# Batch 0's by-key scores on row strips, and the deviation factors on the projected queries

## What is computed

```python
q = split_heads(layernorm(x) @ Wq + bq); k = split_heads(y @ Wk + bk); v = split_heads(y @ Wv + bv)
w = softmax(einsum('bhqd,bhkd->bhqk', q, k) / sqrt(32)); o = merge_heads(w @ v) @ Wo + bo
x = x + tanh(g_xattn) * o
z = layernorm(x); s = max(amax(|z|), 1e-6) / 127; zq = clip(round(z / s), -128, 127)
x = x + tanh(g_ffn) * ((zq @ Wq8.T) * s * w_scale + bias)
```

## Time and profile before

| | |
|---|---|
| median of 3 runs | 812.34 us (811.54 to 814.0) |
| profiled execution | 812.89 us |
| its span, first to last instruction | 811.1 us |
| PE busy | 780.3 us (96%) |
| mean granted TensorE clock | 0.987 |
| POOL, DVE, ACT busy | 66%, 67%, 75% |

### The profile page before, as it was taken

One profiled execution on the slowest core, in us unless ns is written; L12 is line 12 of the kernel. 1 busy time (PEld: TensorE's weight loads), 2 busy tenths in 40 slices (PEclk: granted clock), 3 DMA queues, 4 the chain that ended last, 5 costly groups with the idle time before them and its releaser, 6 DMA issues.

```text
span 811.1 us, 16246 instructions
## 1 busy us (share of the span) xinstructions
PE 780.3 (96%) x5890; PEld 533.0 (66%) x5890; DVE 539.8 (67%) x849; ACT 610.8 (75%) x844; POOL 533.9 (66%) x554
## 2 busy tenths in 40 slices
PE   8897799999999999999999999999999999999996
PEld 6665366667667766766766676676667677666563
DVE  5864567567666756767676676766667665656568
ACT  5773577878687887768778686877868787787785
POOL 4844447585685857578485756949576694845588
PEclk9998899999999999999999999999999999999999
DMA  8998698779768786986878797686779768656722
GB/s 289 309 269 243 198 277 241 221 196 308 230 186 254 223 261 197 267 243 212 259 214 239 197 304 228 190 268 210 260 200 281 221 175 252 188 161 186 208 67 103
DMA packets 119503, 183.21 MB, mean 226 GB/s; under 512 B 37632, under 2 KB 47232, under 8 KB 117376
## 3 DMA queue, kind: packets, MB, share of 16 engines
q1 hardware_dynamic: 92352, 133.33, 53.3%
q10 hardware_dynamic: 27072, 48.84, 22.6%
HBM read 123.91 MB, written 58.22 MB: 225 GB/s over the span
## 4 chain that ended last, share of the span: by engine, by line
PE 76%; POOL 5%; issue 5%; DVE 4%; DMA 3%; ACT 3%; SPq 2%; ACTq 1%; DVEq 0%; POOLq 0%
PE bank_b L428 24%; PE bank_a L428 16%; PE scores L483 7%; PE sum_ps L510 6%; PE scores L502 6%; PE pv_ps L514 6%; PE bank_a L558 4%; PE bank_b L558 2%; SPq L231 2%; PE bank_a L533 1%; DMA k_rows<-k_parts 1%; PE scores L428 1%; DMA rstd_rows<-ln_rstd 1%; POOL o_lo_end L1585 1%; POOL x_rstd L1559 1%
## 5 line engine op out<-in xcount | busy, mean ns | idle before, releaser
L1585 POOL TENSOR_TENSOR o_lo<-on,o_hi 128x512 fp32r<-128x512 f32 x48 | 62.3, 1298 | 139.0 <-ACT o_hi L915 139.0
L1236 DVE TENSOR_REDUCE row_max<-scores 128x16 f32<-128x1920 f32 x64 | 137.9, 2155 | 22.6 <-PE scores L483 22.4
L895 ACT ACTIVATE probs<-scores 120x2048 f32<-120x2048 f32 x64 | 120.2, 1877 | 28.9 <-PE scores L502 28.9
L1248 DVE SCALAR_TENSOR_TENSOR q_parts<-bank_b,bq_c,q_parts 128x512 fp32r<-128x512 f32 x45 | 33.5, 744 | 108.9 <-ACT q_parts L857 108.9
L1540 POOL TENSOR_TENSOR xt<-xt,rstd_b 128x512 f32<-128x512 f32 x60 | 92.3, 1576 | 12.3 <-DMA xt<-in_x_t 10.6
L1593 POOL TENSOR_TENSOR x<-x,gbias_r 128x512 f32<-128x512 f32 x64 | 83.0, 1300 | 20.2 <-ACT cen L921 19.1
L483 PEld LDWEIGHTS scores<-k_sb,q_sb 32*128 32x128 f32 x1952 | 60.5, 187 | 52.4 <-issue 46.5
L1581 POOL TENSOR_TENSOR x<-x,gbo_r 128x512 f32<-128x512 f32 x64 | 83.3, 1313 | 0.8 <-DMA x<-in_x 0.7
L502 PE MATMUL scores<-q_stack,k_stack 128*120 128x512 f32 x256 | 72.8, 406 | 8.3 <-DMA k_stack<-k_rows 7.6
L1598 POOL TENSOR_TENSOR x<-x,u_sb 128x512 f32<-128x512 f32 x56 | 72.7, 1299 | 4.7 <-DVE u_sb L1324 4.5
L428 PE MATMUL bank_b<-xt_hi,wq_hi 128*128 128x512 f32 x188 | 74.9, 399 | 0.0
(11 more groups left out here) (235 smaller groups left out, 1953.1 us busy)
## 6 DMA issues: line engine op xcount, KB each, us to landing
q_stack<-q_rows ACTq DMA_DIRECT2D x183, 256.0 KB, 4.4
q_rows<-q_parts SPq DMA_DIRECT2D x62, 512.0 KB, 5.4
xt<-in_x_t SPq DMA_DIRECT2D x16, 1024.0 KB, 7.9
x<-in_x SPq DMA_DIRECT2D x64, 256.0 KB, 4.5
out_x<-x SPq DMA_DIRECT2D x61, 256.0 KB, 3.2
x_in<-in_x SPq DMA_DIRECT2D x60, 256.0 KB, 5.1
k_stack<-k_rows SPq DMA_DIRECT2D x96, 120.0 KB, 4.6
k_rows<-k_parts SPq DMA_DIRECT2D x28, 240.0 KB, 2.9
```

Of the source, the lines that this page charges most:

```text
L895: act.activation(probs[0:KEYS], scores[0:KEYS], ACT.Exp, scale=SCALE).then_inc(p_ready, 1)
L1236: dve.tensor_reduce(row_max[:].rearrange("p (t r) j -> p r t j", r=ROWG)[:, :, :, j], scores[:, :, 0:QT * KEYS].rearrange("p r (t k) -> p ...
L1585: pool.tensor_tensor(o_lo[i % 2][j], on[:], o_hi[i % 2][j].bitcast(F32), ALU.subtract).then_inc(o_split, 1)
```

## The change

Three things are changed.

1. **Batch 0's by-key scores without HBM.** `scores_by_key0(j)` takes the queries and keys of batch 0 as they lie, four heads on four strips of 32 rows. Three passes of four products (high by high, high by low, low by high) and a fourth with the maxima (8 rows of each strip, picked by `pick0`) add up in the four PSUM banks. The stores and stacks of batch 0 go away (`store_q(0, j)`, `stack_q(0, j)`, `stack_k(0, h)`), and `copy_max` and `spread_max` of batch 0 with them; the high parts are taken by ACT (`split_high0`), the low parts by DVE (`split_low0`). `low_k(0, 0)` to `low_k(0, 3)` are still needed for batch 1 and move later; SP's list ahead of step 1 is written anew.
2. **x unscaled in every batch.** `scale_x` is gone from POOL. DVE multiplies the projected queries with the deviations in the PSUM bank (`scale_q(n, j, bank)`), between `project_q` and `bias_q`; `bias_q` now waits for `q_scaled`.
3. **Places.** In the first quarter of a step, `scale_q(b, 0)` and `split_low(b, 0)` stand ahead of `quant_max(e, 2)`. In the third, `scale_q(b, 2)` stands between `quant_max(m, 0)` and `quant_max(m, 1)`. On PE the wait for `q_split(b, 0)` moves behind `quantised_layer(e, 1)`.

```diff
             def bias_q(n, j, bank):
...
-                act.wait_ge(q_done, nth(n, DT, j))
+                act.wait_ge(q_scaled, nth(n - 1, DT, j))
...
+            def scores_by_key0(j):
+                pe.wait_ge(qk0_split, nth(j, 2, 1))
+                q, k = q0_parts(j), k0_parts(j)
+                for p, (a, b) in enumerate(((0, 0), (0, 1), (1, 0))):
+                    for r in range(ROWG):
+                        pe.matmul(scores[0:KEYS, r], k[a][STRIPS[r]], q[b][STRIPS[r]], start=p == 0, stop=False)
...
+                for r in range(ROWG):
+                    rows = slice(r * DH, r * DH + PAIR)
+                    ins = pe.matmul(scores[0:KEYS, r], pick0[rows, j:j + 1].broadcast_to([PAIR, KEYS]), max0_t[rows],
+                                    start=False, stop=True)
...
+            def scale_q(n, j, bank):
+                dve.wait_ge(q_done, nth(n, DT, j))
+                if n == 1:
+                    dve.wait_ge(rstd1_copied, 1)
+                    dve.tensor_tensor(bank[:], bank[:], rstd1, ALU.mult).then_inc(q_scaled, 1)
+                else:
+                    dve.wait_ge(rstd_landed, 16 * (n - 1))
+                    by_tile = bank[:].rearrange("q (t p) -> q t p", t=QT)
+                    dve.tensor_tensor(by_tile, by_tile, rstd_b[:].rearrange("q (p t) -> q t p", t=QT),
+                                      ALU.mult).then_inc(q_scaled, 1)
...
                 if is_batch(m):
                     quant_max(m, 0)
+                if is_batch(b):
+                    scale_q(b, 2, bank_a)
+                if is_batch(m):
                     quant_max(m, 1)
                     quant_factors(m, 0)
...
-            def scale_x(n, c):
...
-                if is_batch(n):
-                    scale_x(n, 0)
-                    scale_x(n, 1)
-                    scale_x(n, 2)
-                    scale_x(n, 3)
```

More of the change, by code:

```diff
@@ L349, in _ @@
             load(rest_landed, ident_b[:], consts_bf16)
+            load_x(2, 0)
+            load_x(2, 1)
+            load_ctx(1)
+            load_xt(2)
+            store_k(0, 0)
+            store_k(0, 1)
+            stack_k(1, 0)
+            load_x(2, 2)
+            load_x(2, 3)
+            store_q(1, 0)
+            store_k(0, 2)
             load_x(3, 0)
@@ L352, in _ @@
             store_rstd(2)
+            load_rstd(2)
+            store_q(1, 1)
+            store_k(0, 3)
+            load_x(3, 2)
+            load_x(3, 3)
+            stack_k(1, 1)
+            store_q(1, 2)
+            store_k(1, 0)
+            load_x(4, 0)
+            store_rstd(3)
+            store_q(1, 3)
+            store_k(1, 1)
+            load_residual(0, 0)
+            load_residual(0, 1)
+            load_residual(0, 2)
+            load_x(4, 1)
+            load_residual(0, 3)
+            load_ctx(2)
+            load_xt(3)
             def step(i):
@@ L407, in step @@
                 if is_batch(f):
-                    load_rstd(f)
                     load_xt(f)
-            for i in range(0, B):
+            for i in range(1, B):
                 step(i)
@@ L486, in scores_by_query, with turn_max0 @@
                 ins.then_inc(a_done, 1)
+            def turn_max0(bank):
+                pe.wait_ge(max_split, 1)
+                for t in range(QT):
+                    ins = pe.matmul(bank[:, t * P:(t + 1) * P], max0_sp[:, t * ROWG:(t + 1) * ROWG].rearrange("p r c -> p (r c)"),
+                                    ident_r[:], start=True, stop=True)
+                ins.then_inc(max_turned, 1)
             def turn_max(n, bank):
@@ L601, in step @@
                     pe.wait_ge(v_ready, nth(b, 1))
-                if keys_next or values_next and i > 1 or not is_batch(n):
+                if not is_batch(n):
                     pe.wait_ge(q_split, nth(b - 1, DT, 0))
@@ L605, in step @@
                     quantised_layer(e, 1, bank_a if is_batch(n) else bank_b)
+                if keys_next or values_next and i > 1:
+                    pe.wait_ge(q_split, nth(b - 1, DT, 0))
                 if keys_next:
@@ L1347, in step @@
                 if i == 0:
+                    split_low0(2)
                     x_statistics(2, 2)
@@ L1499, in _ @@
             maxima(0, 1)
+            split_low0(0)
             x_statistics(1, 3)
@@ L1502, in _ @@
             maxima(0, 2)
-            maxima(0, 3)
-            low_max(0)
             low_x(1, 0)
             low_x(1, 1)
+            maxima(0, 3)
+            low_max0()
             low_x(1, 2)
             low_x(1, 3)
+            split_low0(1)
             low_ctx(1)
@@ L1611, in step @@
                 if i == 0:
+                    low_k(0, 2)
                     x_rstds(2)
@@ L1656, in step @@
                 low_o(i, 3)
+                if i == 0:
+                    low_k(1, 1)
                 if i == LAST - 1:
```

266 lines of the change are left out of this document (132 added, 134 removed).

## The result

| | before | changed |
|---|---|---|
| median | 812.5 us (811.54 to 814.0, 4 runs) | 849.8 us (848.61 to 850.48, 4 runs) |
| ratio | | 1.0456 (95%: 1.0436 to 1.0476) |
| span of the profiled execution | 811.1 us | 847.7 us |
| PE busy | 780.3 us (96%) | 779.8 us (92%) |

The account below looks back on a forecast made before the run. PE, busy 96% of the span, was taken to bound the kernel. Step 0 -12.0, third quarters +18.0, step 14 +0.5 and the moved wait -3.0 made +3.5 us: 816.4 us profiled, 815.8 us median, range 804 to 825.

Parts of the forecast that it names:

- Step 0: Step 0, batch 0's scores without HBM: a gain of 12 us, 8 to 16, from a ceiling of 18 us.
- rival D: Batch 0's by-key products in step 0: the four strips do not overlap, +11 us, 826.8 us; chance 0.05.
- (b): First quarter of step 0: scale_q(1, 0) stands behind gating wo and the statistics; PE waits some 1.3 us.
- (d): Fourth quarter of step 0: scale_q(1, 3) stands behind the statistics and two row gatings; 2.0 us.
- (e): End of step 0: maxima, turn_max, and scale_q(2, 0) behind the 8-bit weights' cast and the statistics; 1.8 us.
- (c): Step 0: wo_lo holds POOL for 3.47 us between low_o(0, 0) and low_k(0, 3); 0.8 us for the quarters around.
- The duration of the scaling: scale_q on DVE: taken as 0.68 us from a like-shaped row, with bounds of 0.60 us and twice that.
- The third quarter: Ordinary steps: scale_q(b, 2) behind quant_max(m, 0) makes PE wait 1.35 us in steps 2 to 13, 16.2 us.
- The first quarter: Ordinary steps, ahead of scores_by_query(b, 0): scaling, bias and handovers take 1.5 to 1.6 of 1.9 us; no wait.
- Rival C: Ordinary steps: half clock follows each of fourteen new 1.35 us gaps, 21 us more, 837 us; chance 0.03.
- The second and fourth quarters: Ordinary steps: a transpose ahead of attend gives 2.4 us against 1.6 needed; low parts 0.1 us later; zero cost.
- The moved wait: PE's wait for q_split(b, 0) behind quantised_layer(e, 1): six gaps close, -3.3 us, 0.3 given back, -3.0 us.

## Why the prediction was wrong, step by step

**Step 0: right.** Forecast -12, and `scores_by_query(2, 0)` near 90.5; measured 12.5 us, at 90.07. By its terms, on PE, DVE and POOL:

```profile
58.76 0.50 PE L511 MATMUL scores<-o_hi 32*120 32x512 f32 x4
59.09 0.41 PE L511 MATMUL scores<-o_lo,o_hi 32*120 32x512 f32 x4
59.32 0.41 PE L511 MATMUL scores<-o_hi,o_lo 32*120 32x512 f32 x4
59.56 0.42 PE L517 MATMUL scores<-o_hi_end,pick 8*120 8x512 f32 x4
...
63.39 1.06 PE L539 MATMUL sum_ps<-probs,ones_f 120*32 120x512 f32 x8 [0.42 <-ACT probs L938]
...
66.77 1.17 PE L488 MATMUL scores<-k_sb,q_sb 32*128 32x120 f32 x32 [1.46 <-ACT q_sb L869]
...
49.65 0.68 DVE L1301 TENSOR_TENSOR o_lo<-u_tail,o_hi 128x512 fp32r<-128x512 f32 x1
50.25 0.28 DVE L1303 TENSOR_TENSOR o_lo<-k_sb,o_hi 128x120 fp32r<-128x120 f32 x1
...
62.44 1.68 DVE L1301 TENSOR_TENSOR o_lo<-u_tail,o_hi 128x512 fp32r<-128x512 f32 x1
64.03 1.36 DVE L1303 TENSOR_TENSOR o_lo<-k_sb,o_hi 128x120 fp32r<-128x120 f32 x1
65.31 0.69 DVE L1309 TENSOR_TENSOR bank_a<-bank_a,x 128x512 f32<-128x512 f32 x1
...
63.53 1.72 POOL L1656 TENSOR_TENSOR o_lo<-on,o_hi 128x512 fp32r<-128x512 f32 x1
```

The four strips overlap: sixteen products in 1.2 us, so rival D is out. Term (b) was 1.3 us and is 0.84; (d) was 2.0 us and is nothing, (e) was 1.8 us and is 1.45. But the third quarter, for which there was only a part of the 0.8 us of (c), costs 1.46. There `scale_q(1, 2)` stands behind batch 0's last low parts, which take 1.68 and 1.36 us while POOL works; the same two take 0.68 and 0.28 us in the second quarter (49.65 and 50.25), when it does not. The second of them begins half a microsecond behind POOL's `low_o` at 63.53 and ends 0.14 us behind its end. That is what the prediction weighed for (b) by the Trainium skill (SBUF — State Buffer, on the shared port pair), two quarters later; in the first quarter it shows in one low part alone, 0.79 us instead of 0.28. The sum came out near the forecast by luck, from errors that cancel.

**The duration of the scaling: the step that failed.** "The same shape with SBUF as output is 0.68 us ... I take 0.68, since the input side is the same." It was not. The row's operand, `inv_sum`, lies in the bank's order; the diff shows `rstd_b[:].rearrange("q (p t) -> q t p", t=QT)`, and this was read past. What the runs showed in its place is 1.05 to 1.12 us, for a step of 16 bytes in the SBUF operand, and 0.70 us without that step, wherever the result goes. The upper bound of 1.2 us stood there, next to the truth, but it was not carried into the range: with it the 0.3 us "to spare" in the other quarters would have been gone. With the operand in a row, and the scaling where the change has it, the time is 823.9 us, inside the range.

**The third quarter: mechanism right, size off.** Forecast 1.35 us, measured 2.1. With the operand in a row it is 1.33 to 1.35, so the whole excess is the stride: 0.35 us in the instruction itself, and some 0.4 us because `split_low(b, 1)` and `maxima(b, 1)` of the second quarter end later by as much, and the chain by way of `normalise_o` and POOL begins there. The prediction held the start of that chain fixed. Twelve steps: 25 us instead of 16.

**The first quarter: "no wait, with 0.3 us to spare" was false.** 1.05 us in even steps and 0.35 in odd ones, 8 us in all, of which 1.0 stands ahead of step 2 and is counted with step 1 below. In even steps DVE is still at `ctx_lo` when the bank is ready (338.90 in the rows above, against 333.25 before with the bank ready at 334.4). With 0.70 us for the scaling there is no wait in either.

**The clock: a rival with 3 in 100 that came true in part.** Rival C asked whether waits of 1.35 us halve the clock, and for those the answer is no in the one profiled execution that has them (1.34 us, full speed in all twelve steps). That gaps of this size leave the clock alone, as the prediction had it, does not carry over to those that came: half clock followed six of the twelve of 2.1 us. It did not ask what a longer wait would bring. Six steps by 1.5 to 1.6 us; 9.4 us in all, by the stretches from the third to the fourth `scores_by_query`.

**The second and fourth quarters**: forecast zero. From the second `scores_by_query` to the next stage it is 1.91 us instead of 1.78. Less the waits counted elsewhere, the second quarters of steps 2 to 13 are 1.1 us longer than before, and the fourth 3.1. The profile names no releaser for it (0.16 us of idle time ahead of the quantised layer, put down to "issue"). In the kernels with 0.70 us for the scaling the 1.91 us are 1.78 again, so it too came with the stride; by which path is not shown. **Step 1**: +3.1 us where 0.9 was forecast, with the 1.0 us ahead of step 2 in it.

**The ends**: step 14 and what follows cost 2.7 us where 0.9 and 0.5 were forecast, and in step 13 PE waits 1.2 us anew for DVE's `max_sp`.

The sum: -12.5 (step 0) + 3.1 (step 1) + 25.1 (third quarters) + 7.0 (first quarters, from step 3 on) + 9.4 (clock) + 4.2 (second and fourth quarters) + 1.2 (step 13) + 2.7 (the end) - 3.6 (the moved wait, by the first quarters of steps 2 to 13) = 36.6 us, which is what lies between the two spans.

**The moved wait: right**, -3.0 forecast; alone it gave 2.5 us by the medians, 3.7 us by the even steps of the profiled execution.

## What to carry to other kernels

Before a duration is taken from another row, compare the access patterns of every operand, not only engine, shape and memory: the cost here sat in a `rearrange` of an operand that is the same size. An instruction put into the path between an engine and the one that bounds the kernel should stand ahead of everything on its queue that waits for a third engine or a DMA; the four cases here (behind `quant_max`, behind low parts, behind statistics of a tile still loading, behind a residual) each cost PE 1 to 2.6 us. And where waits of PE grow, their price is not linear in these traces, since half clock follows the longer ones more often.

## What the hardware showed that was not expected

- A VectorE product of two fp32 operands of 512 columns takes 0.70 us with its SBUF operand in a row and 1.05 to 1.14 us with a step of 16 bytes; a step of 512 bytes in its PSUM input and output costs nothing (0.70 us).
- In the profiled executions of all twelve kernels, from step 0 on, waits of TensorE of 1.24 to 1.37 us were followed by full speed every time (27 times), those of 1.44 to 1.50 us by half speed 3 times of 11, of 1.73 to 1.77 us 2 times of 3, of 2.02 to 2.11 us 7 times of 13, of 2.38 us 11 times of 12, of 2.55 to 2.71 us 2 times of 3, and of 5.0 us and more 4 times of 4. In the third quarter of ordinary steps half speed then cost 1.5 to 1.6 us each time.
- A store of 512 single fp32 elements, instead of 128 pieces of four, kept SP waiting 8.4 us for it instead of 1.1, and with it the load behind; an x tile came late for that, and PE waited 1.8 us.
